# Graph layers on one core: 432 of the 1568 edge tiles gathered beside the making of the relation table

## The reference, cut to what matters

```
dst = minimum((6250 * uniform(200000) ** 2.0).astype(int32), 49999); src, dst sorted by dst
edge_type = randint(200000, 0, 8)
h    = layernorm(x)
hx   = einsum('ni,rio->rno', h, weight)                  # 8 relations, weight 8 x 256 x 256
agg  = segment_sum(hx[edge_type, src], dst, 6250)
x    = x + agg * 0.5**0.5 + h_bias + (h @ loop_weight) * 0.5**0.5
```

## Time and profile before

| | |
|---|---|
| median of 3 runs | 5592.78 us |
| the profiled execution | 5587.87 us, span 5586.1 us, mean granted TensorE clock 0.797 |
| busy | TensorE 4589.4 us (82%), GpSimd 3321.6 (59%), VectorE 2560.5 (46%), ScalarE 1535.1 (27%) |
| table stage | 78.17 to 504.69 us |
| relation sums, gathers issued | 504.69 to 2471.91 us |
| attention inputs, TensorE | 2567.67 to 2682.0 us |

### The profile page before, as it was taken

One profiled execution on the slowest core, in us unless ns is written; L12 is line 12 of the kernel. 1 busy time (PEld: TensorE's weight loads), 2 busy tenths in 40 slices (PEclk: granted clock), 3 DMA queues, 4 the chain that ended last, 5 costly groups with the idle time before them and its releaser, 6 DMA issues. The chain is left out here.

```text
span 5586.1 us, 72963 instructions
## 1 busy us (share of the span) xinstructions
PE 4589.4 (82%) x18025; PEld 2918.7 (52%) x18026; DVE 2560.5 (46%) x8476; ACT 1535.1 (27%) x3400; POOL 3321.6 (59%) x3405
## 2 busy tenths in 40 slices
PE   3998888887888788963588888876769999997698
PEld 1554333333333333323477777765347777775466
DVE  6562333333333222233355555544875544444682
ACT  1332000000000000001244444434467644442132
POOL 1113777777777777750477777770357777776121
PEclk9998555566656655555699999987889999998798
DMA  3323333333333433320333323225155544443001
GB/s 138 128 122 132 105 105 105 105 105 106 105 105 109 108 105 105 105 76 11 69 61 61 61 60 60 60 54 186 63 153 174 162 136 137 134 136 101 13 1 46
DMA packets 312438, 545.32 MB, mean 98 GB/s; under 512 B 74735, under 2 KB 212734, under 8 KB 305810
## 3 DMA queue, kind: packets, MB, share of 16 engines
q0 software_dynamic: 141088, 319.86, 22.1%
q1 hardware_dynamic: 171092, 222.51, 12.3%
HBM read 449.02 MB, written 93.08 MB: 97 GB/s over the span
## 5 line engine op out<-in xcount | busy, mean ns | idle before, releaser
L959 PE MATMUL e_sums<-e_ring,e_onehot 128*128 128x257 f32 x3136 | 1660.2, 638 | 307.8 <-DMA e_ring<-table,erow 225.1
L713 POOL DMA_INDIRECT e_ring<-table,erow x1568 | 1490.8, 951 | 477.9 <-issue 381.3
L959 PEld LDWEIGHTS e_sums<-e_ring,e_onehot 128*128 128x128 f32 x3136 | 734.3, 287 | 1228.9 <-issue 907.1
L1901 POOL DMA_INDIRECT t_source<-source_rows,t_index x848 | 808.5, 953 | 271.0 <-issue 232.2
L1070 POOL DMA_INDIRECT e_ring<-table,esrc x800 | 802.9, 1004 | 243.6 <-issue 156.1
L914 DVE SCALAR_TENSOR_TENSOR big<-e_sums,within,big 128x257 f32 x196 | 95.1, 485 | 1289.9 <-PE e_sums L959 1289.9
L1146 PE MATMUL e_total<-e_loads,e_times 128*128 128x256 f32 x2176 | 536.2, 381 | 0.0
L1157 PE MATMUL e_sums<-e_ring,e_onehot 128*128 128x256 f32 x1600 | 449.5, 391 | 81.1 <-DMA e_ring<-table,esrc 76.0
L2050 PE MATMUL t_raw<-big,t_w 128*128 (+1 forms) x1600 | 428.1, 428 | 8.6 <-issue 8.6
L1146 PEld LDWEIGHTS e_total<-e_loads,e_times 128*128 128x128 f32 x2176 | 399.0, 190 | 65.7
L920 DVE TENSOR_SCALAR e_onehot<-ramp,edst 128x128 f32<-128x128 f32 x1568 | 344.4, 294 | 95.3 <-PEq L106 67.3
(11 more groups left out here) (382 smaller groups left out, 5365.4 us busy)
## 6 DMA issues: line engine op xcount, KB each, us to landing
table<-r_stage SPq DMA_DIRECT2D x49, 1024.0 KB
e_loads<-table SPq DMA_DIRECT2D x384, 128.0 KB
t_near<-near_rows SPq DMA_DIRECT2D x106, 256.0 KB
e_ring<-table,erow POOLq DMA_INDIRECT x1568
m_outputs<-first_outputs SPq DMA_DIRECT2D x49, 512.0 KB, 4.8
first_outputs<-t_stage SPq DMA_DIRECT2D x96, 256.0 KB
t_source<-source_rows,t_index POOLq DMA_INDIRECT x848, 2.4
e_ring<-table,esrc POOLq DMA_INDIRECT x800
```

Source lines behind the costliest of these rows:

```text
L713: eng.indirect_dma_start(ring[:, t % BODY, 0:D], None, table, bass.IndirectOffsetOnAxis(ap=b.erow[:, t:t + 1], axis=0)).then_inc(gathered[ ...
L959: eng.matmul(sums[g % SUMS][:, 0:ACCW], onehot[t % ONEHOTS][:, :], ring[:, t % BODY, :], start=(t % GROUP == 0), stop=(t % GROUP == GROUP ...
L1901: eng.indirect_dma_start(source[s][:, q, :], None, a.source_rows, bass.IndirectOffsetOnAxis(ap=index[s][:, q:q + 1], axis=0)).then_inc(gat ...
```

## The change

432 tiles (EARLY), the ones with the lowest targets, are gathered during `relation_table` and not in `relation_sums`. They do not use the table: the normalized rows themselves are written to HBM (`rows1`) at the start of the phase, the tile's rows `rows1[src]` are gathered, and the one-hot matrix has a column for each pair of node and relation, 16 nodes by 8 relations. A group is four tiles, and its sum is added to a window of 16 nodes x 8 relations by 256. The 48 windows of these sums stand in `b.x`, which is normalized in place (28 windows by VectorE, 21 by ScalarE), written out, cleared, and loaded again from HBM later. After six windows the table's own input comes back from `rows1` by DMA. All 432 one-hot matrices are made by VectorE. Between them, after every second tile, VectorE does one step of the sort, of which 26 steps are done before; and the products of the table rotate through three PSUM banks.

In `relation_sums` 1136 tiles remain. Six chunks (8 windows of the early sums each) are transposed and multiplied by the relations' weights there, 16 transposes and 16 products of 256 columns per chunk, spread over tiles 8 to 104. The PSUM buffers of the group sums go from four to two. `attention_inputs` goes from two to four buffers, keeps TensorE two windows ahead, drops one of ScalarE's two copies and gathers the products of 32 and of 17 windows in a bank each. `far_edges` loads its own list of targets, and `sparse_table` loads one list less. A further scope with its own barrier encloses the first layer.

```diff
@@ constants: more index work, weights loaded here, scr_edst in another form for the first tiles
+            eng.dma_start(erows[:, :], m["edst_rows"]).then_inc(loaded, 16)
...
+            eng.dma_start(b.esrc[:, :], m["src_cols"][:, 0:EARLY]).then_inc(loaded, 16)
             eng.dma_start(b.x[:, :, :], m["x"].rearrange("(w p) d -> p w d", p=P)).then_inc(loaded, 16)
+            for k in range(KH):
+                eng.dma_start(b.weights[:, k, :, :], ...).then_inc(b.weighted, 16)
+            eng.dma_start(b.loopw[:, :, :], ...).then_inc(b.weighted, 16)
...
+            p.did(eng.scalar_tensor_tensor(b.edst[:, 0:EARLY], ediff[:, :], float(ENODES), eslot[:, :], ALU.is_lt, ALU.mult))
@@ relation_table, SyncE
+            for j in range(NW // RUN):
+                eng.wait_ge(normed[0], MINE * (j + 1))
+                eng.wait_ge(normed[1], (RUN - MINE) * (j + 1))
+                eng.dma_start(runs[j], b.x[:, RUN * j:RUN * (j + 1), :]).then_inc(written, 16)
+            eng.wait_ge(written, 16 * (NW // RUN))
...
+            for w in range(NW):
+                eng.wait_ge(evacuated, (w + 1) * OUTS)
+                eng.dma_start(table[w], stage[w % 2][:, :]).then_inc(stored[w % 2], 16)
+                if DIRECT + HELD <= w + HELD < NW:
+                    bring(w + HELD)
@@ relation_table, GpSimd
-            for w in range(NW):
-                wait_if(eng, transposed, w - 1)
-                eng.tensor_scalar(xn[w % 2][:, :], b.x[:, w, :], b.mean[:, w:w + 1], b.rstd[:, w:w + 1], ...)
+            eng.wait_ge(written, 16 * (NW // RUN))
...
+            for t in range(EARLY):
+                if t >= RING:
+                    eng.wait_ge(summed, t - RING + 1)
+                    eng.sem_inc(cleared, 1)
+                eng.indirect_dma_start(ring[:, t % RING, 0:D], None, m["rows1"], bass.IndirectOffsetOnAxis(
+                    ap=b.esrc[:, t:t + 1], axis=0)).then_inc(gathered[t % RING], 16)
@@ relation_table, VectorE (the sort's stages are the same; it yields after each)
+            def add(g):
+                w = eng.value_load(b.ebase[0:1, g:g + 1], min_val=0, max_val=EWINDOWS - 2)
+                eng.wait_ge(summed, (g + 1) * EGROUP)
+                wait_if(eng, added, 4 * g)
+                for side, mask in ((0, b.ewithin), (1, b.ebeyond)):
...
+                    eng.scalar_tensor_tensor(window, sums[g % 2][:, 0:D], mask[:, g:g + 1], window, ALU.mult, ALU.add)
+                    eng.scalar_tensor_tensor(count, sums[g % 2][:, D:ACCW], mask[:, g:g + 1], count, ALU.mult, ALU.add)
+            for w in range(NW):
+                if w % RUN < MINE:
+                    eng.tensor_scalar(b.x[:, w, :], b.x[:, w, :], b.mean[:, w:w + 1], b.rstd[:, w:w + 1], ...)
...
+            for _ in range(TABLE_FIRST):
+                next(sort_steps)
+            eng.wait_ge(written, 16 * (NW // RUN))
+            eng.wait_ge(transposed, DIRECT)
+            eng.memset(b.x[:, :, :], 0.0).then_inc(zeroed, 1)
...
+            for t in range(EARLY):
+                wait_if(eng, summed, t - RING + 1)
+                eng.tensor_scalar(onehot[t % RING][:, :], b.ramp[:, 0:P], b.edst[:, t:t + 1], None, ALU.is_equal)
+                if t % 2 == 1:
+                    next(sort_steps, None)
+                if t % EGROUP == EGROUP - 1 and t // EGROUP >= 1:
+                    add(t // EGROUP - 1)
@@ relation_table, TensorE
+            def gather_sum(t):
+                g = t // EGROUP
+                if t % EGROUP == 0:
+                    wait_if(eng, added, 4 * (g - 1))
+                eng.wait_ge(matched, t + 1)
+                eng.wait_ge(gathered[t % RING], 16 * (t // RING + 1))
+                eng.matmul(sums[g % 2][:, 0:ACCW], onehot[t % RING][:, :], ring[:, t % RING, :], ...)
...
+            for w in range(NW):
+                eng.wait_ge(copied, w + 1)
+                if w + 1 < NW:
+                    turn(w + 1)
+                for c in range(OUTS):
+                    multiply(w, c)
+                    for t in early_at(w, c):
+                        gather_sum(t)
+                        if t in FLIPPED:
+                            flip(FLIPPED.index(t))
@@ relation_sums: fewer tiles, and the early sums multiplied by the weights
-            for t in range(NT):
+            for t in range(TILES):
...
-    SUMS = 4
+    SUMS = 2
...
+            eng.wait_ge(flipped, CHUNKS * FILLS)
+            eng.dma_start(b.x[:, :, :], m["x"].rearrange("(w p) d -> p w d", p=P)).then_inc(restored, 16)
...
+            def put(c, f):
+                if f < FILLS:
+                    wait_if(eng, laid, c * FILLS + f)
+                    for k in range(KH):
+                        for two in range(2):
+                            mm = eng.transpose(turning[:, ...], b.x[:, c * RELS + 2 * f + two, k * P:(k + 1) * P], b.ident[:, :])
+                    mm.then_inc(flipped, 1)
+                    return
...
+                for r in (2 * (f - FILLS), 2 * (f - FILLS) + 1):
+                    for k in range(KH):
+                        mm = eng.matmul(product[:, 0:D], turned[:, k, :].rearrange("p (n r) -> p r n", r=RELS)[:, r, :],
+                                        b.weights[:, k, r, :], ...)
@@ attention_inputs
-        xn = [sb(f"g_xn{s}", [P, D]) for s in range(2)]
-        xt = [sb(f"g_xt{s}", [P, KH, P]) for s in range(2)]
+        xn = [sb(f"g_xn{s}", [P, D]) for s in range(WAYS)]
...
+            for w in range(AHEAD):
+                turn(w)
+            for w in range(NW):
+                if w + AHEAD < NW:
+                    turn(w + AHEAD)
...
+                    mm = eng.matmul(product[half][:, at:at + HE], b.xt[:, k, w * P:(w + 1) * P], wgat[:, k, :], ...)
```

More of the change, by code:

```diff
@@ L21 @@
 RELS = 8
-FILLED = 6
+FILLED = 9
 E = 200000
@@ L375, in relation_table @@
         kept = sem("r_kept")
+        cleared = sem("r_cleared")
+        gathered = [sem(f"r_gathered{s}") for s in range(RING)]
+        matched = sem("r_matched")
+        summed = sem("r_summed")
+        added = sem("r_added")
         block = ctx.enter_context(nc.Block())
@@ new lines, in add @@
+            def add(g):
[3 more added lines that the diff above has]
+                for side, mask in ((0, b.ewithin), (1, b.ebeyond)):
+                    window = b.x[:, bass.ds(w + side, 1), :].rearrange("p a c -> p (a c)")
+                    count = b.counted[:, bass.ds(w + side, 1)]
+                    eng.scalar_tensor_tensor(window, sums[g % 2][:, 0:D], mask[:, g:g + 1], window,
+                                             ALU.mult, ALU.add).then_inc(added, 1)
+                    eng.scalar_tensor_tensor(count, sums[g % 2][:, D:ACCW], mask[:, g:g + 1], count,
+                                             ALU.mult, ALU.add).then_inc(added, 1)
@@ L581, in relation_sums @@
     ONEHOTS = BODY
-    SUMS = 4
+    SUMS = 2
     SLOTS = (3, 11)
-    assert BODY * (2 + ASKED[-1] // 2 + 6) < NT
+    TILES = NT - EARLY
+    GROUPS = TILES // GROUP
+    CHUNKS = EWINDOWS * ENODES // P
+    FILLS = RELS // 2
+    PUTS = 2 * FILLS
+    PUT = lambda n: BODY // 2 + 2 * n
+    put_at = {PUT(n): divmod(n, PUTS) for n in range(CHUNKS * PUTS)}
+    assert BODY * (2 + ASKED[-1] // 2 + 6) < TILES and PUT(CHUNKS * PUTS) < BODY * 20
     with Phase(nc) as ctx:
@@ L917, in _, with join @@
+            def join(c, g):
+                eng.wait_ge(multiplied, c + 1)
+                wait_if(eng, added, 2 * g)
+                if joined.n:
+                    joined.settled()
+                joined.did(eng.tensor_tensor(b.acc[:, c, :], b.acc[:, c, :], product[:, 0:ACCW], ALU.add))
             sorting = sort()
-            for t in range(NT):
+            summing = 0
+            for t in range(TILES):
                 wait_if(eng, summed, t - ONEHOTS + 1)
-                eng.tensor_scalar(onehot[t % ONEHOTS][:, :], b.ramp[:, 0:P], b.edst[:, t:t + 1], None,
+                eng.tensor_scalar(onehot[t % ONEHOTS][:, :], b.ramp[:, 0:P], b.edst[:, EARLY + t:EARLY + t + 1], None,
```

620 lines of the change are left out of this document (398 added, 222 removed).

## The result

The changed kernel takes 5271.7 us (median of 4 runs, 5270.6 to 5272.8) against 5591.2 us for the kernel before (now the median of four runs): a ratio of 0.9425, with an interval of 0.9408 to 0.9441, so 319.5 us less. The forecast was 5294 us. The profiled execution has a span of 5270.3 us and a mean clock of 0.837.

The account below looks back on a forecast made before the run. GpSimd's gathers, 1.255 us per step, were taken to pace the relation sums. 8 + 277.4 (table stage) + 3 (scope) + 15 - 542.3 - 60 = -298.9 us from 5587.9, plus 4.9 to the median: 5294 us, range 5190 to 5400.

Parts of the forecast that it names:

- The gathers that go: Relation sums: 432 tiles taken out at 1.255 us each, 542.3 us less, all on the path.
- The chunks: Relation sums: transposing and multiplying the early sums costs 15 us, ends 0 and 65; 34 us per chunk at half clock.
- Ahead of the table stage: In `constants`: more loads, small VectorE operations, stores and SyncE loads cost 8 us, bounds 4 and 15.
- The prelude: Table stage before the early tiles: normalizing 28 windows, preparing the sort, 24 sort stages and clearing `b.x`, together 66.4 us.
- The loop: Table stage's 432 early tiles: 619 us with held-up gathers plus 11 us, so 630 us, ends 550 and 783.
- The hold-up: Early tiles: gathers wait for VectorE's sort operations with both operands in SBUF, 0.45 x 0.5 = 0.22 us per gather.
- The coupling of ring, flips and stores: Early tiles: TensorE and GpSimd wait for each other now and then, and table stores share DMA queues; 11 us added.
- The one row: Profile before, gather at 1843.44 us: 1.65 us, not 0.95, beside a VectorE operation with both operands in SBUF.
- not held up: Rival for the early tiles: VectorE does not delay gathers, loop 560 us, time 5224 us; chance 0.24.
- VectorE the bound: Rival for the early tiles: VectorE's operations are delayed as gathers are, loop 695 us, time 5389 us; chance 0.17.
- Half clock: Rival for the early tiles: TensorE's clock stays at 0.5 to 0.63, loop 1087 us, time 5751 us; chance 0.03.
- Attention inputs: Nothing waited for but the first load: 60 us saved, between 50 (half clock, 64 us) and 82 (full clock, 32 us).

Follow-up runs that it names:

- the two experiments with extra operations: Changed kernel plus 680 VectorE operations in the relation sums: tensor-tensor with two SBUF operands, 5399.6 us (0.9667); reductions with one SBUF operand, 5264.6 us (0.9423).
- the experiment: Changed kernel with the attention inputs as before (two buffers, product's copies in VectorE's round, ScalarE's second copy): 5330.4 us (0.9528).

## Why the prediction was right

**The gathers that go.** 432 steps of 1.255 us was right: the 1136 left take 1431.3 us for 1135 steps, 1.261 each. The chunks, forecast at 15 us, cost 1431.3 - 1135 x 1.2554 = 6.4. From 820 to 910 us, in the chunks' stretch, TensorE was busy 28 of every 30 us at a clock of 0.84 to 0.94, so the case of half clock, with its 34 us per chunk, did not come.

**Ahead of the table stage.** Forecast 8 us, ends 4 and 15; measured 14, nearly the upper end. The first small store was issued 5.6 us later than before (42.77 against 37.19). From there to the first load back it took 6 us longer, a term that the sum did not have, and the work behind took 2.4 us longer.

**The prelude.** 66.4 forecast, 158.42 - 92.12 = 66.3 measured. Its parts were each within some 3 us: the clearing took 10.51 us where 49 small ones would have been 13.3.

**The loop.** Forecast 630 us, measured 767.50 - 158.42 = 609. The mechanism was right, and both of its sizes too large. The hold-up was 0.22 us per tile over 342 tiles, 75 us in all; the trace has 67.9. Its two factors were right as well: of the first 342 gathers 142 (0.42, forecast 0.45) took over 1.0 us, and these 0.47 us more than 0.945 on average (forecast 0.5). The coupling of ring, flips and stores was put at 11 us; no cost of it is seen. The gathers' pace is their own mean and some 0.31 us in every part of the loop (1.403 for 1.098 in tiles 100 to 200, 1.257 for 0.953 behind the sort). 432 x 1.2554 + 67.9 = 610 us is the whole loop. (GpSimd's eight gathers of head start shorten it and the last products lengthen it; the two are of about the same size.)

**The one row.** One row of before, the gather of 1.65 us, carried the choice between 560 and 630 us for the loop. In the changed kernel single gathers reach 2.25 us, the mean beside the sort is 1.142 (forecast above 1.1) and behind it 0.954, and the two experiments with extra operations showed the cause by itself. The rival "not held up", with 5224 us, falls: its sign is a loop below 580 us with gathers of 0.95, and only the kernel with the sort ahead has these (541 us, 0.955).

**VectorE the bound.** This rival (5389) falls in the form it had: VectorE is busy 384.5 of 609 us, and waits 173.6 us for group sums. What is true in it is that less work on VectorE shortens the loop by some 23 us, through the gathers.

**Half clock.** The clock was 0.98 in the loop. TensorE had waits of 38 us for gathers in 609, and these did not lower it.

**The tail and the scope.** 774.89 - 767.50 = 7.4 us against 7.5. The scope's 3 us can't be separated: the next phase's first operation follows the last gather by 9.2 us, where it was 11.0.

**Attention inputs.** Forecast 60 us saved, between 50 and 82; the two traces have 56.5, the experiment 57.6. TensorE works from 2300.45 to some 2358 us, 1.173 us per window:

```profile
2300.45 1.54 PE L1655 MATMUL g_turned<-ident,g_xn 128*128 128x128 f32 x6 [10.90 <-DMA g_att<-in_att_dst]
...
2353.41 0.87 PE L1668 MATMUL g_product<-g_wgat,big 128*128 128x16 f32 x4
2354.12 0.67 PE L1655 MATMUL g_turned<-ident,g_xn 128*128 128x128 f32 x2
...
2355.76 2.58 PE L1668 MATMUL g_product<-g_wgat,big 128*128 128x16 f32 x12
```

The half-clock case was right in its clock, though a window takes 1.173 us and not the 1.30 of the forecast (64 us in all). The argument "never idle, then full clock", by which it could have been 32, was wrong here. The 60 us stood between the two cases; that it came out within 4 us is luck in part, as the half-clock case alone gave 50.

**The sum.** The forecast was 22 us too high. The terms, each as measured in the traces less forecast: constants +6, the loop -21, the chunks -9, the attention inputs +3.5, the step between the phases -4.5, and 8 us that the stages behind gave back and no step had; that makes -17. The rest is the level of the runs: the median stands 1.4 us above the profiled span here, where 6.7 went into the forecast (1.8 around the span and 4.9 to the median).

## What to carry to other kernels

A gather on GpSimd costs its own duration and a fixed issue, and both can be read from a row; but before work is put beside gathers, look what VectorE does there: an operation with both operands in SBUF holds a gather up by about what is left of it, and a second one right behind it mostly holds it up as well (28 gathers of 36). If an operand can stand in PSUM, the gather keeps its time; if not, apart is better than back to back (an excess of 47.1 against 67.9 us). When a stage's start is moved forward, look which engine's own work then ends last.

## What the runs showed of the hardware

- A pair of VectorE operations of 0.68 us with two SBUF operands stretches an indirect gather of 128 rows from 0.945 us up to 2.2 us; reductions of the same length with one SBUF operand leave it at 0.949 in the mean, and so do tensor-tensor operations with one operand in PSUM that write 512 columns to SBUF.
- TensorE stood at clock 0.50 (1.2 GHz) through 50 us in which it was busy 50.00 us, with transposes and products of 16 columns. Before the change it was busy 28.70 of 50 us there, at the same 0.50. Being busy without a gap did not bring the clock up.
- From the first of some small stores to HBM to the first load back it took 13.2 us with six stores, and 7.2 with three; the time was the same with 2.3 MB of weights ahead in the queue or behind.
- A one-hot matrix made by VectorE (a tensor-scalar operation) stood 5.69 us beside GpSimd's clearing of 9.72 us and ended with it, in one kernel, while the sort's tensor-tensor operations ahead of it had run at their usual 0.42 us beside the same clearing.
